# A decoder layer's cross-attention: the softmax denominators' reciprocals taken once per sum, spread over all partitions by DMAs, and four more quarters of key tiles summed in fours

## What is computed

```python
x = layernorm(x + linear_attention(x))          # 16 heads of 32, elu + 1 features
q, k, v = x @ wq.T, ctx @ wk.T, ctx @ wv.T      # 16 heads of 32
dots = q @ k.T * 32 ** -0.5                     # per head 1024 x 2048
attn = softmax(dots)                            # = exp(dots - max) / sum(exp(dots - max))
x = layernorm(x + (attn @ v) @ wo.T + bo)
x = layernorm(x + mixture_of_experts(x))        # 8 experts, 2 per token, capacity 640
```

## Time and profile before

| | before |
|---|---|
| median of 3 runs | 1900.84 us (1900.61 to 1901.95) |
| the profiled execution's own time | 1900.81 us |
| its span, first to last instruction | 1899.0 us |
| TensorE busy | 1865.9 us (98%) |
| VectorE busy | 1251.7 us (66%) |
| ScalarE busy | 892.8 us (47%) |
| GpSimd busy | 823.9 us (43%) |
| granted TensorE clock, mean | 0.990 |

### The profile page before, as it was taken

One profiled execution on the slowest core, in us unless ns is written; L12 is line 12 of the kernel. 1 busy time (PEld: TensorE's weight loads), 2 busy tenths in 40 slices (PEclk: granted clock), 3 DMA queues, 4 the chain that ended last, 5 costly groups with the idle time before them and its releaser, 6 DMA issues.

```text
span 1899.0 us, 26632 instructions
## 1 busy us (share of the span) xinstructions
PE 1865.9 (98%) x9992; PEld 1277.1 (67%) x9992; DVE 1251.7 (66%) x2362; ACT 892.8 (47%) x1600; POOL 823.9 (43%) x745
## 2 busy tenths in 40 slices
PE   9999999999999999999999999999969999999998
PEld 8886787788555555555445545544439998899986
DVE  6675574277787888888778778778653444444447
ACT  4312323221665666666556556546724433344333
POOL 4002201000687888888667667665021233222232
PEclk9999999999999999999999999999979999999999
DMA  8003525684767585748543524441234554444544
GB/s 284 23 1 116 186 98 177 205 245 141 152 142 159 124 198 125 168 100 176 128 125 93 129 69 127 112 112 62 84 124 132 139 130 121 113 110 128 149 103 158
DMA packets 124497, 250.11 MB, mean 132 GB/s; under 512 B 11312, under 2 KB 29504, under 8 KB 119680
## 3 DMA queue, kind: packets, MB, share of 16 engines
q1 hardware_dynamic: 109696, 187.56, 33.2%
q0 software_dynamic: 14672, 60.85, 15.6%
HBM read 148.46 MB, written 62.42 MB: 111 GB/s over the span
## 4 chain that ended last, share of the span: by engine, by line
PE 86%; DVE 12%; issue 1%; ACT 0%; DMA 0%; POOL 0%; SPq 0%; DVEq 0%; POOLq 0%; ACTq 0%
PE banks L1197 38%; PE banks L1493 12%; PE banks L1392 11%; PE banks L1362 10%; DVE max L1709 9%; PE banks L1381 9%; PE banks L1413 4%; PE banks L1203 2%; PE banks L1293 1%; DVE den_c L1728 1%; PE banks L1370 0%; ACT y_nat L2114 0%; DMA xg<-x_rows,tok 0%; DMA raw<-in_wk_t 0%; POOL xg L2252 0%
## 5 line engine op out<-in xcount | busy, mean ns | idle before, releaser
L1709 DVE TENSOR_REDUCE max<-banks 128x1 f32<-128x512 f32 x1024 | 627.9, 682 | 128.7 <-PE banks L1362 127.5
L2214 POOL TENSOR_TENSOR probs<-probs,probs 128x512 f32<-128x512 f32 x464 | 583.0, 1293 | 231.5 <-PE banks L1392 231.5
L2095 ACT ACTIVATE probs<-banks 128x512 f32<-128x512 f32 x1024 | 521.2, 608 | 258.6 <-PE banks L1381 258.0
L1362 PE MATMUL banks<-k_stack,q_stack 98*128 98x512 f32 x1024 | 428.3, 426 | 0.2
L1381 PE MATMUL banks<-q_stack,k_stack 98*128 98x512 f32 x1024 | 376.7, 398 | 2.5 <-ACT probs L2095 2.5
L1362 PEld LDWEIGHTS banks<-k_stack,q_stack 98*128 98x128 f32 x1024 | 191.5, 187 | 191.7 <-DVE max L1709 108.5
L1392 PE MATMUL banks<-probs,v_grp 128*32 128x512 f32 x2048 | 250.5, 601 | 0.0
L1381 PEld LDWEIGHTS banks<-q_stack,k_stack 98*128 98x128 f32 x1024 | 191.7, 188 | 60.2 <-ACT probs L2095 16.8
L2261 POOL DMA_INDIRECT y_rows<-eo,tok x35 | 69.3, 1981 | 173.4 <-DVE eo L1922 118.3
L1909 DVE TENSOR_TENSOR hid_lo<-hid,hid_hi 128x640 fp32r<-128x640 f32 x64 | 52.7, 824 | 127.6 <-ACT hid_hi L2161 127.6
L1392 PEld LDWEIGHTS banks<-probs,v_grp 128*32 128x32 f32 x2048 | 60.0, 109 | 108.4 <-issue 102.3
(11 more groups left out here) (266 smaller groups left out, 2800.7 us busy)
## 6 DMA issues: line engine op xcount, KB each, us to landing
k_stack<-k_parts SPq DMA_DIRECT2D x144, 256.0 KB, 5.2
probs<-probs POOLq DMA_DIRECT2D x36, 1024.0 KB, 10.0
w_raw<-in_L_ffn_w SPq DMA_DIRECT2D x16, 2048.0 KB, 8.4
q_stack<-q_parts SPq DMA_DIRECT2D x48, 256.0 KB
v_grp<-v_rows SPq DMA_DIRECT2D x48, 256.0 KB, 3.4
raw<-in_ctx_t SPq DMA_DIRECT2D x8, 1024.0 KB, 6.4
k_parts<-out_hi SPq DMA_DIRECT2D x32, 256.0 KB, 2.6
k_parts<-out_lo SPq DMA_DIRECT2D x32, 256.0 KB, 3.1
```

What stands on the lines that cost most here:

```text
L1362: nc.tensor.matmul(out, queries_of(t)[:, j, tile_of(k)], keys_of(t)[0:STK + SHIFT, j, mc * HALF:(mc + 1) * HALF], start=True, stop=True) \
L1709: V.reduce_max(max4[:, tiles_of(t), :, :][:, k, j, mc:mc + 1], bank(bank_of["max", t, mc, k, j]), AX.X) \
L2095: S.activation(probs_of(t, s)[:, j, :], bank(bank_of["score", t, s, j]), ACT.Exp, scale=SCALE) \
L2214: G.tensor_tensor(a[:, j, :], a[:, j, :], b[:, j, :], ALU.add).then_inc(pair_added.sem, 1)
```

## The change

The reciprocals. For turns 0 to 13 (`spread(t)`) the 8 pieces are gone. The 512 different sums of each head, which lie in one row of `den_c`, are moved by four DMAs to 32 partitions each (`spread_den`, into `den_s`, 128 x 16), VectorE takes one reciprocal of that (`invert_spread`), one DMA stores it to `den_rows` in DRAM (`store_den`), and four DMAs bring it back, broadcast to the 32 rows of each head (`return_den`). The stages are put 1, 3, 3 and 4 blocks behind `copy_den`, and the four divisions 6, 6, 7 and 7 blocks behind it; for turn 6 all four 6 blocks behind it. All nine DMAs are issued by SyncE. Turns 14 and 15 are left as they were.

The sums. `LATER_FOURS` gets quarter 1 of turns 9 and 11 and quarters 0 and 1 of turn 12.

```diff
-LATER_FOURS = {(8, 0), (8, 1), (10, 1), (13, 0), (13, 1)}
+LATER_FOURS = {(8, 0), (8, 1), (9, 1), (10, 1), (11, 1), (12, 0), (12, 1), (13, 0), (13, 1)}
+SPREAD_DIVISIONS = (6, 6, 7, 7)
...
+        den_rows = nc.dram_tensor("den_rows", (HG, HALF), F32).ap()
...
+        den_s = put("den_s", [P, HG * HALF // P])
...
+        def spread(t):
+
+            return t < LAST - 1
...
                 if s == MT - 1:
                     do("copy_den", t)
+                    if spread(t):
+                        for wait, stage in ((1, "spread_den"), (3, "invert_spread"), (3, "store_den"), (4, "return_den")):
+                            later.append((clock + wait, do, (stage, t)))
+                        for k in range(HT):
+                            later.append((clock + (6 if t == B * NG - 2 else SPREAD_DIVISIONS[k]), divide, (t, k)))
+                        continue
...
+            def invert_spread(t):
+                dve.wait_ge(*den_spread[t])
+                V.reciprocal(den_s[:, :], den_s[:, :]).then_inc(inverted.sem, 1)
...
-                pool.wait_ge(*inverted[t, (k + 1) * SHARE - 1])
+                pool.wait_ge(*(den_back[t] if spread(t) else inverted[t, (k + 1) * SHARE - 1]))
...
+            def spread_den(t):
+                sp.wait_ge(*den_copied[t])
+                for j in range(HG):
+                    Q.dma_start(den_s[j * DH:(j + 1) * DH, :],
+                                den_c[j * DH:j * DH + 1, :].rearrange("r (p f) -> r p f", p=DH)) \
+                        .then_inc(den_spread.sem, 16)
+
+            def store_den(t):
+                sp.wait_ge(*inverted[t])
+                Q.dma_start(den_rows.rearrange("j (p f) -> (j p) f", p=DH), den_s[:, :]).then_inc(den_stored.sem, 16)
+
+            def return_den(t):
+                sp.wait_ge(*den_stored[t])
+                for j in range(HG):
+                    Q.dma_start(den_c[j * DH:(j + 1) * DH, :], den_rows[j].partition_broadcast(DH)) \
+                        .then_inc(den_back.sem, 16)
```

More of the change, by code:

```diff
@@ L457, in program @@
             "invert": lambda t, q: (inverted,),
+            "spread_den": lambda t: (den_spread,),
+            "invert_spread": lambda t: (inverted,),
+            "store_den": lambda t: (den_stored,),
+            "return_den": lambda t: (den_back,),
             "divide": lambda t, k: (divided,),
@@ L1971, in _ @@
                     "xq": lambda *key: split_part("xq", *key), "ctx_k": lambda *key: split_part("ctx_k", *key),
-                    "add_pair": add_pair, "invert": invert, "zero_counts": zero_counts, "rows": rows,
+                    "add_pair": add_pair, "invert": invert, "invert_spread": invert_spread, "zero_counts": zero_counts, "rows": rows,
                     "parts": parts, "row_root": row_root, "row_shift": row_shift, "fold": fold, "fold_turn": fold_turn, "logits": logits,
```

5 lines of the change are left out of this document (4 added, 1 removed).

## The result

The changed kernel takes **1921.03 us** (median of 6 runs, 1916.12 to 1924.64) against 1900.72 (6 runs, 1900.03 to 1901.95). The ratio on record is 1.0103, 95% interval 1.0093 to 1.0114 (the two medians divide to 1.0107). Slower, where no change was predicted, and 16.5 us above the upper end of the range. Its runs lie 8.5 us apart, those of before 1.9. The profiled execution took 1917.55 us, with a span of 1915.7.

What follows compares the result with a forecast made beforehand. TensorE was taken to set the pace, with VectorE full only in some blocks of batch two. Terms -3.6 - 1.15 - 0.3 + 4.4 = -0.6 us against 1900.81 gave 1900.2 us; range 1895.8 to 1904.5.

Steps and rivals of the forecast that it cites:

- 112 reciprocals become 14: VectorE's fewer reciprocals gain 3.6 us (0 to 3.6), only in blocks where VectorE is full; nothing in batch one.
- Four groups of ones less: On TensorE, 93 groups become 89: 3.4 us less 2.25 taken back in turns 9, 11, 12; gain 1.15 (0.5 to 3.4).
- The hold in turn 8: ScalarE's `copy_den` waits for turn 6's divisions behind GpSimd's pair sum, delaying the next numerators: 4.4 us lost (3.6 to 5).
- The DMAs: Nine more SyncE issues a turn cost 0; the spread, about 1.9 us by its nearest row, has at least 11.9 us.
- Side work one block later: In block 0 of turn 9 ScalarE keeps only the denominators' copy, both `x2` moving on: 0.3 us gained (0 to 0.6).
- The rivals: No hold: 1895.8 us, chance 0.1; chain right about `den_c`: near 1885, chance 0.03; spread landing late: 1914, chance 0.07.
- The one on the slower side: The spread lands over 11.9 us after issue, stopping maxima and TensorE in 14 turns; 1914 us at one over, chance 0.07.

Runs made afterwards that it cites:

- e8: The change with VectorE's copy of the last row of counts written as a sum over an axis of length one (turns 9, 12, 14); 1907.76 us.
- e1: The change with its spread reciprocals alone, the four added quarters of sums of four taken back; 1906.56 us.
- e7: The change with turn 6's reciprocal left in four pieces and none of the four new quarters; 1901.68 us.
- e10: e7 with VectorE's copy of the counts written as a sum over an axis of length one; 1899.64 us.
- e14: The change with turn 6's reciprocal in pieces and VectorE's copy as a sum over an axis of one, all four new quarters kept; 1902.96 us.
- e3: The change without quarters 0 and 1 of turn 12; 1909.52 us.
- e9: The change with repeated matmuls ahead of the matmuls that wait in turn 8, turn 11 and blocks 2 and 4 of turn 12; 1913.19 us.
- e4: The change, but in turns 9, 11 and 12 GpSimd waits for each pair sum before beginning the next; 1916.07 us.
- e5: The change with turn 6's reciprocal left in four pieces, so that its divisions stand where they stood; 1915.61 us.

## Why the prediction was wrong, by its own steps

The largest miss is a cost that stands in none of its terms. The terms "112 reciprocals become 14" and "four groups of ones less" took VectorE's side steps to last as long as before wherever they land. In turn 12 the new timing put a copy 0.12 us behind the start of GpSimd's sums, and that, with all that followed and 1.0 us of the same kind in turn 9, cost 13.3 us (e8). The rest is gains that were booked and did not come, and a hold that cost more than its bounds.

- **"112 reciprocals become 14"**, -3.6: mis-sized. Plain blocks stayed at 5.95 and 6.80, as said, and several full blocks came out as read: block 2 of turn 11 takes 6.81 (6.8 predicted), block 1 of turn 10 8.93 (8.8), block 2 of turn 14 7.55, and turn 12 gains 1.1 in e1 (1.0). But turn 13 gave 0.1 where 0.5 was booked, and turn 9, booked at -0.3, costs 2.0 in e7 and 1.0 even in e10. Over turns 8 to 14 e7 takes 0.3 us more than before, e10 0.5 less. The step asked only what VectorE has *too much*, not where its steps land once it is early.
- **"Four groups of ones less"**, -1.15: this step failed. Turn 12's floor of 27.4 us for four blocks was 28.3 at best (e8: 6.23, 6.80, 6.76, 8.49), and against the reciprocals alone, which had already brought 29.4, two moved groups of 0.85 cost more than that gives. Turn 11 was priced at -0.35; it cost 1.2 in the change's profiled execution and 3.0 in e14, most of it in a block at a lower clock where TensorE waits instead of multiplying by ones. The hold of 5 us needed these groups gone as well: e1 and e3, which keep turn 12's, don't have it.
- **"The hold in turn 8"**, +4.4: mechanism right, size short. The copy came 4.3 us later, and with the clock kept up (e9) turn 8 takes 74.4, 4.1 over before. What the term lacked is the clock: 1.9 us more here (76.3), 2.6 to 2.8 in e1, e3 and e4. Measured whole it is 5.4 us (e5), over the bound of 5.
- **"The DMAs"**, 0: right for the reciprocals' own. The spread lands in 2.2 us, and VectorE never waited for it. The store took 5.4 and not 1.9; GpSimd waited for the return in three turns, and none of them got longer. But with the new quarter in turn 11 another small DMA, of `shift_rows`, lands late, and TensorE waits for it: 0.2 us in the change, 1.8 in e9.
- **"Side work one block later"**, -0.3: blocks 0 and 1 of turn 9 went from 15.61 to 14.78 together, 0.8 gained, beyond the bound of 0.6 but too little to matter.
- **The rivals**: none was it. The one on the slower side was a late landing; a VectorE held by GpSimd was on no list, though the trace of before shows it, 1.21 us for a step of 0.16 in turn 14. The range held the hold's bounds and the gains' but had no term for a clock that no row shown of the loop before had under 1. Its own bounds give 1897.4 to 1903.3, not 1897.2 to 1903.2, which changes nothing.
- **Luck**: e14 mends both holds and takes 1902.96 us, inside the predicted range. That is no confirmation: by the prediction's own sum a kernel without a hold takes 1895.8. Of the 5.05 us of gains nothing is left there; e14 is 2.1 over its group's before (1900.86).
- The **scatter** of the changed kernel, 8.5 us, was not taken apart. For the same code, turn 8 takes 76.3 to 77.2 us, and turn 11 59.5 in e5, 60.1 in the change and 61.9 in e4; the granted clock of block 3 of turn 11 is 1.00, 0.82 and 0.84 there. So whether and how long the clock stays down varies from run to run.

## What to carry to other kernels

When work is removed from an engine that is not the bound, ask what its remaining steps will now run beside: a small copy or two-input product on VectorE that used to finish ahead of GpSimd's sums can be held by them, for one sum or, as here behind the issue of a DMA, for four; a reduction in the copy's place was not. Price a hold of TensorE as the wait plus a refill at half clock, which may or may not come, and before taking matmuls out of TensorE ask whether it has anything else to do there; if not, they may be what keeps its clock up.
